# Weight splits beside the second block's tiles, the first block's units two at a time, and the state update ahead of the head norm

## The chip, the cores and the metric

The kernel runs on one core of one Trainium2 chip. A core has five engines with instruction queues of their own that meet through semaphores: TensorE (PE, matmuls into PSUM banks), VectorE (DVE), ScalarE (ACT), GpSimd (POOL) and SyncE (SP, which here only issues DMAs). The metric is the device time of one run in microseconds (us); lower is better.

## The reference

The input x is 4 x 1024 x 512 in float32. What is computed:

```python
xn = layernorm(x)
out = x + attn(xn) + ffn(xn)
# attn: an mLSTM layer and its MLP
h_in = rmsnorm(xn, norm1_w)
q, k, v = h_in @ wq, h_in @ wk, h_in @ wv        # 8 heads, 32 columns of q and k, 64 of v
i_pre, f_pre = cap(h_in @ w_ig + b_ig), cap(h_in @ w_fg + b_fg)   # cap(z) = 15 tanh(z / 15)
Fcum = cumsum(log_sigmoid(f_pre)); Dmat = causal(Fcum[t] - Fcum[s] + i_pre[s]); m = max(Dmat)
C = (q @ k.T / sqrt(32)) * exp(Dmat - m)
h = (C / max(|sum(C)|, exp(-m))) @ v
x1 = xn + (sigmoid(h_in @ w_og) * headnorm(h) * mh_w) @ w_out
h2 = rmsnorm(x1, norm2_w)
attn = x1 + (silu(h2 @ w_gate) * (h2 @ w_up)) @ w_down            # 512 -> 2048 -> 512
# ffn: weights looked up from 16 values by index, 512 -> 1376 -> 512
ffn = (silu(xn @ lut[gate_idx].T) * (xn @ lut[up_idx].T)) @ lut[down_idx].T
```

## The kernel before

**Tiling.** The 4096 tokens are 8 blocks of 512 (four batches, two halves each). Every float32 product is made as three matmuls of parts: `hi` and `lo` (the rest that `hi` leaves) of both sides, hi x hi, hi x lo, lo x hi (`split`). ScalarE makes a `hi` by a copy to fp32r, and GpSimd or VectorE the `lo` by a subtraction.

**Stages.** A block has a *front* (gate logits, projections q/k, v and output gate into banks A and B, transposes, and the rows of the gates with two scans on VectorE), and then 16 MLP *tiles*. A tile t has on TensorE a gate pass, an up pass and the down pass of tile t-1, 12 matmuls of 512 columns each; ScalarE does tanh and `hidden_hi`, VectorE the product (`th`, `hm`), GpSimd `hidden_lo`. The tiles that run behind a block's front are those of the block before it, and between their passes stand, in tiles 0 to 7, the block's own eight recurrence *units* (128 tokens and four heads each), then the head transposes (`ho_T`), in tiles 8 and 9 the output projection, in tile 10 the transposes of h2, and at tile 15 those of the next block's input (`x_T`). The order is written out by hand in each engine's program; each step waits on counting semaphores.

**A unit.** TensorE: exponents (L723, bank A), scores (L729, bank B), values (L737 from the state `kv`, L740 from `ct`), state (L747). VectorE: mask (`ar`, L1536), weights (`ct`, L1543), `tt` and `hr` (L1551, L1554: the heads), update and state (L1562, L1567), and after every second unit the head norm (`norm_1`, L1573 to L1590), whose inverse root (`rh`) GpSimd makes before `norm_2` scales and gates `hn`. ScalarE: `qbd` (L1184) and the exponential (L1192).

**The first block** (`FIRST`) has no tiles beside its units, so they stand alone: unit after unit, and then its output projection, x1 and the second block's input transposes. Meanwhile the MLP weights are split: for each of 16 tiles a load of 768 KB (gate, up and down in one), `mlp_hi_` on ScalarE, `mlp_lo_` on GpSimd, and a store of 1.5 MB to `mlp_parts`; four of them in the first front, eight beside the units, the last four in the second block's front (`split(0)` to `split(3)`), these through the buffer `raw_gu`. The second block's tiles (`SECOND`) then reload the weights from `mlp_parts` (`load_gu`, `load_dn`, two slots of `gud`), as all later blocks do. The weights of v and the output gate (`vo_w`) share memory with the look-up's tiles (`look_w`) and are reloaded at the end of each looping block.

**The loop and the tail.** Six blocks run in a loop of three passes with two halves; beside their tiles ScalarE and VectorE look up the ghost weights (`look_up`). The tail has the last block's tiles alone and then the ghost FFN of all 8 blocks, which is matmul after matmul.

## Time and profile before

| | |
|---|---|
| Runs, median (lowest to highest) | 2609.22 us (2608.56 to 2611.22), 3 runs |
| Profiled execution: time, span | 2609.44 us, 2607.3 us |
| TensorE busy | 2458.7 us (94%) |
| VectorE, ScalarE, GpSimd busy | 1270.9 (49%), 914.5 (35%), 605.7 (23%) |
| Granted clock of TensorE, mean | 0.973 of full |
| First block's front, units, rest | 22.6 to 67.7, 68.5 to 155.8, 162.3 to 184.3 us |
| Second block's front, its tiles | 184.3 to 253.3, 262.3 to 437 us |

A granted clock of 1.0 is 2.4 GHz, and 0.5 is 1.2 GHz. Busy time of TensorE is counted in time, so the same matmuls look busier at the lower clock. A wait is told by the instruction that waited, its idle time before, and what released it.

### The profile page before, as it was taken

The page shows a single profiled execution, that of the slowest core. Times are in us where ns is not written, and L with a number is a line of the kernel's source. Part 1 is how long each engine was busy: PE and PEld are TensorE (multiplying, and loading weights), DVE is VectorE, ACT ScalarE, POOL GpSimd, SP SyncE. Part 2 cuts the span into 40 slices and gives each one's busy share as a digit, 9 for nine tenths or more (in the row PEclk, how much of TensorE's full clock was granted, in tenths as well). Part 3 has the DMA queues.
Part 4 walks back from the last instruction along what each step waited for, and adds up shares of the span by engine and source line. Part 5 has one row for each costly group of instructions (what it writes and reads, how often), then busy time and mean ns, then how long its engine had stood idle before and what let it go on. Part 6 is the DMA issues. An engine that isn't in the chain of part 4 may idle for free. (4 is left out here: it accounts for less than half of the span.)

```text
span 2607.3 us, 32285 instructions
## 1 busy us (share of the span) xinstructions
PE 2458.7 (94%) x11024; PEld 1986.6 (76%) x11024; DVE 1270.9 (49%) x2185; ACT 914.5 (35%) x1667; POOL 605.7 (23%) x498
## 2 busy tenths in 40 slices
PE   6565999999999999999999999989999999999998
PEld 5344787877777777787777777768888888888887
DVE  5552563577477467557746746754322222222222
ACT  5313212444445353544444535346211111111111
POOL 4532221222122122222213212222111111111111
PEclk9568999999999999999999999999999999999999
DMA  5534645246445544724644554476687678767865
GB/s 219 205 142 148 243 154 198 98 157 234 158 148 190 205 144 161 290 96 159 230 161 143 198 202 145 160 285 224 220 288 272 242 261 290 256 239 278 284 213 199
DMA packets 117333, 530.32 MB, mean 203 GB/s; under 512 B 11280, under 2 KB 11280, under 8 KB 80304
## 3 DMA queue, kind: packets, MB, share of 16 engines
q1 hardware_dynamic: 110544, 515.86, 55.9%
q10 hardware_dynamic: 6624, 12.32, 1.6%
q8 instruction: 96, 1.57, 0.2%
q14 instruction: 69, 0.57, 0.1%
HBM read 440.46 MB, written 87.69 MB: 203 GB/s over the span
## 5 line engine op out<-in xcount | busy, mean ns | idle before, releaser
L1814 POOL TENSOR_TENSOR hidden_lo<-hm,hidden_hi 128x512 fp32r<-128x512 f32 x216 | 287.4, 1331 | 1360.7 <-ACT hidden_hi L972 1360.7
L664 PE MATMUL gate_bank<-act_hi,gud 128*128 128x512 f32 x1728 | 580.2, 397 | 17.1 <-DMA gud<-mlp_parts 9.0
L664 PE MATMUL up_bank<-act_hi,gud 128*128 128x512 f32 x1728 | 591.9, 404 | 0.0
L664 PE MATMUL acc<-gud,hidden_hi 128*128 128x512 f32 x1728 | 541.2, 395 | 16.8 <-POOL hidden_lo L1814 16.8
L1384 DVE SCALAR_TENSOR_TENSOR th<-th,gate_bank 128x512 f32<-128x512 f32 x216 | 147.9, 685 | 516.2 <-ACT th L967 516.2
L664 PEld LDWEIGHTS gate_bank<-act_hi,gud 128*128 128x128 f32 x1728 | 326.5, 189 | 85.4 <-issue 17.9
L664 PEld LDWEIGHTS up_bank<-act_hi,gud 128*128 128x128 f32 x1728 | 324.9, 188 | 79.2 <-issue 13.5
L664 PEld LDWEIGHTS acc<-gud,hidden_hi 128*128 128x128 f32 x1728 | 318.6, 188 | 83.4 <-issue 12.2
L972 ACT ACTIVATE hidden_hi<-hm 128x512 fp32r<-128x512 f32 x216 | 135.9, 629 | 697.9 <-PE acc L664 694.8
L664 PE MATMUL gate_bank<-act_lo,gud 128*128 128x512 f32 x864 | 338.2, 391 | 0.0
L664 PE MATMUL acc<-gud,hidden_lo 128*128 128x512 f32 x864 | 337.6, 391 | 0.0
L664 PE MATMUL up_bank<-act_lo,gud 128*128 128x512 f32 x864 | 337.5, 391 | 0.0
L967 ACT ACTIVATE th<-gate_bank 128x512 f32<-128x512 f32 x216 | 128.7, 596 | 438.4 <-PE gate_bank L664 438.4
L1390 DVE SCALAR_TENSOR_TENSOR hm<-th,up_bank 128x512 f32<-128x512 f32 x216 | 148.6, 688 | 246.8 <-PE up_bank L664 243.2
L1044 ACT ACTIVATE look_w<-look_w,lt,ld 128x512 f32<-128x512 int32 x280 | 216.1, 804 | 0.0
L664 PEld LDWEIGHTS up_bank<-act_lo,gud 128*128 128x128 f32 x864 | 162.5, 188 | 45.5 <-issue 13.4
L664 PEld LDWEIGHTS gate_bank<-act_lo,gud 128*128 128x128 f32 x864 | 163.4, 189 | 33.3
L664 PEld LDWEIGHTS acc<-gud,hidden_lo 128*128 128x128 f32 x864 | 162.4, 188 | 34.3
L1379 DVE COPY_PREDICATED look_w<-look_w 128x512 f32<-128x512 int32 x228 | 182.2, 842 | 10.1 <-ACT look_w L1044 3.9
L1830 POOL TENSOR_TENSOR MX<-mhl,hm 40x1024 fp32r<-40x1024 f32 x32 | 63.6, 1986 | 164.7 <-DVE mhl L1493 156.1
L729 PE MATMUL bank_b<-qbd,qkT 128*128 128x512 f32 x128 | 73.7, 660 | 21.0 <-DVE tt L1562 18.4
L1184 ACT ACTIVATE qbd<-qkT,bdm 128x128 f32<-128x128 f32 x256 | 81.2, 390 | 3.4 <-PE bank_b L729 3.3
...
## 6 DMA issues: line engine op xcount, KB each, us to landing
gud<-mlp_parts SPq DMA_DIRECT2D x128, 1024.0 KB, 5.1
gud<-ghost_parts SPq DMA_DIRECT2D x88, 1024.0 KB, 5.7
gud<-mlp_parts SPq DMA_DIRECT2D x128, 512.0 KB, 3.8
...
mlp_parts<-gud SPq DMA_DIRECT2D x16, 1536.0 KB, 6.0
...
vo_w_hi<-vo_parts SPq DMA_DIRECT2D x12, 1024.0 KB, 5.9
vo_w_lo<-vo_parts SPq DMA_DIRECT2D x12, 1024.0 KB, 9.8
```

What stands on the lines that cost most here:

```text
L664: mm = pe.matmul(dst, l[a], r[c], start=first and k == 0 and n == 0, stop=last and k == len(lhs) - 1 and n == 2)
L729: pe.matmul(B[:], qkT[:, 1, g, toks(j)], qbd[:, :, :], start=True, stop=True)\
L967: act.activation(th[:], GB[:], ACT.Tanh, scale=0.5).then_inc(of.tanh.sem, 1)
L972: act.activation(HH[0][:], hm[:], ACT.Copy).then_inc(of.hid.sem, 1)
L1044: ins = act.activation(level_of(n, what), bit0(), ACT.Identity, bias=lt[:, 2 * what:2 * what + 1], scale=ld[:, what:what + 1])
L1184: act.activation(qbd[:, h, :], qkT[:, 0, g, j * P:(j + 1) * P], ACT.Copy, scale=bdm[:, h:h + 1]).then_inc(act_qbd.sem, 1)
L1379: dve.copy_predicated(level_of(n, lower), mask_of(n, k).bitcast(i32), level_of(n, upper)).then_inc(look_vec, 1)
L1384: dve.scalar_tensor_tensor(th[:], th[:], 1.0, GB[:], ALU.add, ALU.mult).then_inc(of.gated.sem, 1)
L1390: dve.scalar_tensor_tensor(hm[:], th[:], 0.5, UB[:], ALU.mult, ALU.mult).then_inc(of.hm.sem, 1)
L1814: pool.tensor_tensor(HH[1][:], hm[:], HH[0][:].bitcast(f32), ALU.subtract).then_inc(of.low.sem, 1)
L1830: pool.tensor_tensor(MX[0:n, :, :], mhl[0:n, j * P:(j + 1) * P].unsqueeze(1).to_broadcast([n, H, P]), hm32[0:n, 0:H].unsqueeze(2).to_broad ...
```

## The change

In the order of the program:

- **First block.** Its units run two at a time: odd units have their own banks (`ACC[0]`, `ACC[1]`) and tiles (`qbd2`, `ar2`, `ex2`, `ct2` in `first_rows`, which shares memory with `gud`). TensorE and VectorE do unit u+1's exponents and mask ahead of unit u's weights and values. The second block's LayerNorm and input transposes stand among the units. No MLP weight is split here.
- **Second block's front.** Last head transposes, output projection, x1, h2 and its transposes of the first block stand in it. Two MLP tiles are split (`split(0)`, `split(1)`).
- **Second block's tiles.** The other 14 are split in tiles 1 to 15, gate and up apart from down (`part` 0 and 1), through four raw buffers that share memory with `vo_w`; TensorE takes the split weights straight from `gud`, and the stores to `mlp_parts` follow. `vo_w` is stored early and reloaded after the tiles.
- **All blocks.** The state update stands ahead of the head norm. The inverse root of the norm stands ahead of `hidden_lo` on GpSimd. The four `x_T` stand together in tile 15 in banks B, A, gate and up. The down pass of tile 15 follows the next front's logits. In tile 10 the product stands ahead of the third and fourth h2 scaling. The wait for the stored MLP rows moves from VectorE's first step in the front to ScalarE's row copy.
- **Tail.** The first index load is issued ahead of the tail's tiles, and VectorE's wait for the last `vo_w` reload comes after the first product.

VectorE in the first block, second and third unit, before (`bank_a` and `bank_b` are A and B):

```order
L1551 TENSOR_TENSOR tt<-bank_b,rn 128x260
L1554 TENSOR_TENSOR hr<-bank_a,tt 128x260
L1573 SCALAR_TENSOR_TENSOR nm<-hr 128x8
L1576 TENSOR_TENSOR nm<-nm,rn 128x8
L1578 RECIPROCAL sm<-nm 128x8
L1582 TENSOR_TENSOR hn<-hr,sm 128x512
L1586 TENSOR_TENSOR ar<-hn 128x512
L1588 TENSOR_REDUCE nm<-ar 128x8
L1590 TENSOR_SCALAR sm<-nm 128x8
L1562 TENSOR_TENSOR tt<-bank_b,bdm 128x260
L1567 SCALAR_TENSOR_TENSOR kv<-kv,rn,tt 128x260
L1536 TENSOR_TENSOR ar<-bank_a,maskd 128x512
```

And after (`acc` is `ACC[0]` or `ACC[1]`; `first_rows` as output is `ar2` or `ct2`), third and fourth unit:

```order
L1629 TENSOR_TENSOR first_rows<-acc,maskd 128x512
L1637 TENSOR_TENSOR ct<-bank_b,ex 128x512
L1669 SCALAR_TENSOR_TENSOR nm<-hr 128x8
L1672 TENSOR_TENSOR nm<-nm,rn 128x8
L1674 RECIPROCAL sm<-nm 128x8
L1678 TENSOR_TENSOR hn<-hr,sm 128x512
L1682 TENSOR_TENSOR ar<-hn 128x512
L1684 TENSOR_REDUCE nm<-ar 128x8
L1686 TENSOR_SCALAR sm<-nm 128x8
L1646 TENSOR_TENSOR tt<-bank_b,rn 128x260
L1649 TENSOR_TENSOR hr<-bank_a,tt 128x260
L1657 TENSOR_TENSOR tt<-bank_b,bdm 128x260
```

The mask of the next unit has come ahead of this unit's weights; the head norm of the pair before now stands between weights and heads, where before it stood between heads and update.

TensorE from a block's last up pass on (the second block), before:

```order
L664 MATMUL up_bank<-act_hi,gud 128x512
L699 MATMUL bank_b<-ident,xn 128x128 x4
L699 MATMUL bank_a<-ident,xn 128x128 x4
L664 MATMUL acc<-gud,hidden_hi 128x512 x2
L664 MATMUL acc<-gud,hidden_lo 128x512
...
L664 MATMUL acc<-gud,hidden_lo 128x512
L699 MATMUL bank_b<-ident,xn 128x128 x4
L699 MATMUL bank_a<-ident,xn 128x128 x4
L664 MATMUL acc<-gud,hidden_hi 128x512 x2
L664 MATMUL acc<-gud,hidden_lo 128x512
```

And after (`gates_w` are the weights of the next block's logits):

```order
L717 MATMUL up_bank<-act_hi,gud 128x512
L752 MATMUL bank_b<-ident,xn 128x128 x4
L752 MATMUL bank_a<-ident,xn 128x128 x4
L752 MATMUL gate_bank<-ident,xn 128x128 x4
L752 MATMUL up_bank<-ident,xn 128x128 x4
L717 MATMUL acc<-gud,hidden_hi 128x512 x2
...
L717 MATMUL acc<-gud,hidden_lo 128x512
L1010 ISA
L717 MATMUL up_bank<-act_hi,gates_w_hi 16x512
L717 MATMUL up_bank<-act_lo,gates_w_hi 16x512
L717 MATMUL up_bank<-act_hi,gates_w_lo 16x512
```

The four transposes stand together, and the second row of down passes (tile 15's) has left this place for the one behind the logits.

GpSimd in the second block's tiles 8 to 10, before (`rh` is the norm's inverse root, `rs` with one column that of an x1 row):

```order
L1814 TENSOR_TENSOR hidden_lo<-hm,hidden_hi 128x512
L1766 TENSOR_TENSOR rh<-sm,half_pow 128x8
L1814 TENSOR_TENSOR hidden_lo<-hm,hidden_hi 128x512
L1766 TENSOR_TENSOR rs<-ve,half_pow 128x1 x3
L1814 TENSOR_TENSOR hidden_lo<-hm,hidden_hi 128x512
L1766 TENSOR_TENSOR rs<-ve,half_pow 128x1
```

And after (`gud` rows are splits):

```order
L1920 TENSOR_TENSOR gud<-raw_mlp,gud 128x512 x3
L1935 TENSOR_TENSOR hidden_lo<-hm,hidden_hi 128x512
L1920 TENSOR_TENSOR gud<-raw_mlp,gud 128x512 x3
L1887 TENSOR_TENSOR rs<-ve,half_pow 128x1 x3
L1935 TENSOR_TENSOR hidden_lo<-hm,hidden_hi 128x512
L1920 TENSOR_TENSOR gud<-raw_mlp,gud 128x512 x3
L1887 TENSOR_TENSOR rs<-ve,half_pow 128x1
L1935 TENSOR_TENSOR hidden_lo<-hm,hidden_hi 128x512
```

Three splits have come between every `hidden_lo` and what follows it.

The diff, cut to its core:

```diff
         def raw_slot(m):
-            return m % 2 if m < NM - 4 else 2
+            return m % 4 if m >= 2 else 4

         def raw_part(m):
-            return raw_mlp[:, m % 2, :] if m < NM - 4 else raw_gu[:, :, :].rearrange("p a n -> p (a n)")[:, 0:3 * D]
+            raw = raw_mlp[:, m % 4, :] if m >= 2 else raw_gu[:, :, :].rearrange("p a n -> p (a n)")[:, 0:3 * D]
+            return raw.rearrange("p (g n) -> p g n", g=3)
+
+        def raw_loads(m):
+            return 16 * (m + 1 if m < 2 else (m - 2) // 4 + 1)
+
+        def pick(at, u, even, odd):
+
+            return odd if here(at, FIRST) and u % 2 else even
...
+        def xt_bank(at, i):
+            return AB[i % 2] if here(at, PRE) else ACC[2 + i % 2] if here(at, FIRST) else (B, A, GB, UB)[i]
+
...
-                store_mlp(m)
-            for z in range(2):
-                sp.wait_ge(st_parts[z], 16 * (NM // 2))
-            load_gu(MLP, FIRST, 0)
+            store_vo(2)
+            wait(sp, vec_ln, FIRST, 0, f"xn{NB - 1}")
+            load_mlp(0)
+            wait(sp, vec_xT, FIRST, NB - 1, "lo")
+            store_xt(1, XH[1])
+            wait(sp, vec_x1, FIRST, NB - 1, "x1")
+            sp.dma_start(rows_of(x1_rows, 0), XN[0][:]).then_inc(st_x1, 16)
+            sp.wait_ge(mlp_lo[1], 1)
+            load_mlp(1)
+            sp.wait_ge(st_vo, 64)
+            wait(sp, pe_o, SECOND, NB - 1)
+            for m in (2, 3, 4):
+                load_mlp(m)

             def tiles(at):
                 b, half = at
                 mb = previous(at)
...
+                    if here(at, SECOND):
+                        store_gu(t)
+                        if t:
+                            store_dn(t - 1)
+                        if 2 <= t and t + 3 < NM:
+                            load_mlp(t + 3)
+                    elif t + 1 < NM:
                         load_gu(MLP, mb, t + 1)
                     elif here(at, TAIL):
...
+                if here(at, SECOND):
+                    store_dn(NM - 1)
+                    reload_vo(1)
+                    reload_vo(2)
+                    for z in range(2):
+                        sp.wait_ge(st_gu[z], 16 * NM // 2)
+                        sp.wait_ge(st_dn[z], 16 * NM // 2)
+                    load_gu(MLP, at, 0)
...
                     wait(pe, vec_hoT, at, u // 2 - 1, "lo")
                 else:
                     wait(pe, vec_unit, at, u - 1, "heads")
-                pe.matmul(A[:], AL[:, toks(j)], MX[:, g * HG:(g + 1) * HG, :], start=True, stop=True)\
+                pe.matmul(pick(at, u, A, ACC[0])[:], AL[:, toks(j)], MX[:, g * HG:(g + 1) * HG, :], start=True, stop=True)\
                     .then_inc(pe_unit.sem, 1)
                 wait(pe, act_qbd, at, u, "h3")
                 wait(pe, act_qkT, at, NB - 1, "k")
-                if u:
+                if here(at, FIRST):
+                    if u >= 2:
+                        wait(pe, vec_unit, at, u - 2, "update")
+                elif u:
...
+                if not isinstance(at[0], int):
+                    down(MLP, previous(previous(at)), NM - 1, NM - 1)
...
+                if here(at, SECOND):
+                    ho_T(FIRST, NB - 1)
                 q_k_T(at, 0)
+                proj(at, 2)
                 if here(at, SECOND):
                     for i in range(NB):
-                        h2_T(FIRST, i)
-                proj(at, 2)
+                        out_proj(FIRST, i)
                 q_k_T(at, 1)
                 proj(at, 3)

...
                     if stage and t == NM - 1:
-                        x_T(at, 0, XN[1 - at[1]])
-                        x_T(at, 1, XN[1 - at[1]])
+                        for i in range(NB):
+                            x_T(at, i, XN[1 - at[1]])
                     if t:
                         down(MLP, mb, t - 1, NM - 1)
                     for f, a in fill.get((t, 2), []):
                         f(at, a)
-                if stage:
-                    x_T(at, 2, XN[1 - at[1]])
-                    x_T(at, 3, XN[1 - at[1]])
-                    down(MLP, mb, NM - 1, NM - 1)

             pe.wait_ge(pool_const, IDENT_DONE)
             for i in range(NB):
                 x_T(PRE, i, XN[0])
             front(FIRST)
+            unit_1(FIRST, 0)
             for u in range(UNITS):
-                unit_1(FIRST, u)
+                if u + 1 < UNITS:
+                    unit_1(FIRST, u + 1)
                 unit_2(FIRST, u)
                 unit_3(FIRST, u)
-                if u in (2, 4, 6):
+                if u in (3, 5, 7):
                     ho_T(FIRST, u // 2 - 1)
-            ho_T(FIRST, NB - 1)
-            pe.wait_ge(pool_w, 2)
-            for i in range(NB):
-                out_proj(FIRST, i)
-            for i in range(NB):
-                x_T(FIRST, i, XN[1])
+                if u in (4, 5):
+                    for i in (0, 1):
+                        x_T(FIRST, 2 * (u - 4) + i, xn_first)

...
+            def mlp_hi_(m, part):
                 z = m % 2
-                act.wait_ge(ld_mlp[raw_slot(m)], 16 * (m // 2 + 1 if m < NM - 4 else m - (NM - 5)))
+                act.wait_ge(ld_mlp[raw_slot(m)], raw_loads(m))
                 if m >= 2:
-                    act.wait_ge(st_parts[z], 16 * (m // 2))
-                act.activation(W3[:, z, :, 0, :], raw_part(m).rearrange("p (g n) -> p g n", g=3), ACT.Copy).then_inc(mlp_hi, 1)
+                    act.wait_ge((st_gu, st_dn)[part][z], 16 * (m // 2))
+                    wait(act, (MLP.up, MLP.down)[part], FIRST, m - 2)
+                kinds = slice(2, 3) if part else slice(0, 2)
...
+                elif here(at, SECOND):
+                    act.wait_ge(st_x1, 16)
+                    wait(act, vec_h2, FIRST, NB - 1)
+                else:
+                    act.wait_ge(st_mlp[1 - half], b * 16)
...
+                    if t:
+                        hid(MLP, mb, t - 1)
+                        if here(at, SECOND) and t >= 2:
+                            mlp_hi_(t, 1)
+                    tanh(MLP, mb, t, stage)
                     if stage and t < UNITS:
-                        unit(t)
+                        unit(at, t)
+                    if here(at, SECOND) and 1 <= t < NM - 1:
+                        mlp_hi_(t + 1, 0)
                     if stage and t == 10:
...
+                    ho_T(FIRST, NB - 1)
+                    for i in range(NB):
+                        x1_(FIRST, i)
+                    for i in range(NB):
+                        h2_(FIRST, i)
+                    dve.wait_ge(st_x1, 16)
...
+            def units_first():
+
+                at = FIRST
+                clear_state(at)
+                unit_1(at, 0)
+                for u in range(UNITS):
+                    if u + 1 < UNITS:
+                        unit_1(at, u + 1)
+                    weights(at, u)
+                    if u in (2, 4, 6):
+                        norm_1(at, u // 2 - 1)
+                    if u in (3, 5, 7):
+                        norm_2(at, u // 2 - 1)
+                    unit_2(at, u)
+                    unit_3(at, u)
+                    if u == 1:
+                        ln_stats(at, x_raw, 1, 16)
+                    if u == 2:
+                        ln_square(at)
+                    if u == 3:
+                        ln_apply(at, xn_first, 1, x_raw)
+                    if u in (4, 6):
+                        ho_T(at, u // 2 - 2)
+                    if u in (5, 6):
+                        for i in (0, 1):
+                            x_T(at, 2 * (u - 5) + i)
+                norm_1(at, NB - 1)
+                ho_T(at, NB - 2)
+                norm_2(at, NB - 1)
+                wait(dve, vec_norm, at, NB - 1, "gated")
+                for i in range(NB):
...
                             h2_scale(at, 1)
                             h2_lo(at, 0)
-                            h2_scale(at, 2)
                             h2_lo(at, 1)
-                            h2_scale(at, 3)
-                            h2_lo(at, 2)
-                            h2_lo(at, 3)
-                    if not first:
-                        product(MLP, mb, t)
+                    product(MLP, mb, t)
+                    if not stage and t == 0:
+                        for z in range(2):
+                            dve.wait_ge(ld_vo[z], 32 + 32 * HALVES * (BATCH - 1))
+                        bit_0(at, 0)
+                    if stage and t == 10:
+                        h2_scale(at, 2)
+                        h2_scale(at, 3)
+                        h2_lo(at, 2)
+                        h2_lo(at, 3)
                     if stage and t < UNITS:
                         if t in (2, 4, 6):
-                            norm_2(t // 2 - 1)
-                        unit_2(t)
+                            norm_2(at, t // 2 - 1)
+                        unit_2(at, t)
                         if looks(at):
                             look_up(at, steps_taken(half, t))
+                        unit_3(at, t)
                         if t % 2:
-                            norm_1(t // 2)
-                        unit_3(t)
+                            norm_1(at, t // 2)
                         if t in (2, 4, 6):
...
+                for u in range(UNITS):
+                    vw_(at, u)
+                    if u in (1, 3, 5):
+                        mx_(at, u // 2 + 1)
+                    if u in (2, 4, 6):
+                        norm_root(at, u // 2 - 1)
...
+                    if stage and t in (2, 4, 6, 8):
+                        norm_root(at, t // 2 - 1)
+                    if t:
                         hid(MLP, mb, t - 1)
...
+                        if here(at, SECOND) and 1 <= t < NM - 1:
+                            mlp_lo_(t + 1, 0)
                         if t in (1, 3, 5):
-                            mx_(t // 2 + 1)
-                        if first and t < UNITS:
-                            mlp_lo_(4 + t)
-                        if first and t == 5:
-                            ln_root(at)
-                        if first and t == 7:
```

## Rows read from the trace of the kernel before

**Rows 1.** Windows: stretch, us; busy us of PE, PEld, DVE, ACT, POOL; PEclk, DMA share, GB/s.

```profile
68.00:156.00 88.00, 53.32 (x132) 31.50 (x132) 50.50 (x92) 30.17 (x56) 50.11 (x41) 0.54 0.56 209
156.00:184.00 28.00, 17.05 (x68) 13.37 (x68) 17.70 (x41) 2.88 (x5) 5.20 (x7) 0.74 0.34 129
184.00:262.00 78.00, 48.51 (x204) 36.36 (x204) 21.73 (x33) 27.04 (x48) 18.76 (x14) 0.81 0.37 130
262.00:437.00 175.00, 172.86 (x793) 141.37 (x794) 92.13 (x174) 39.57 (x80) 41.19 (x36) 0.99 0.54 192
2000.00:2200.00 200.00, 200.00 (x885) 165.77 (x884) 47.62 (x72) 30.41 (x50) 32.28 (x25) 1.00 0.77 271
```

**Rows 2.** TensorE's waits, 68 to 184: total us, times, longest.

```profile
PE bank_b L729 <- DVE tt L1562: 13.9, 4, 5.2
```

**Rows 3.** TensorE's waits, 184 to 263.

```profile
PE gate_bank L699 <- ACT qkT L1104: 11.4, 2, 9.3
PE gate_bank L664 <- DMA gud<-mlp_parts: 9.0, 1, 9.0
PE bank_b L664 <- ACT th L1121: 6.3, 1, 6.3
```

**Rows 4.** Timeline, first units: start, us, engine, line, form, [idle <- releaser].

```profile
74.62 1.23 PE L737 MATMUL bank_b<-kv,qkT 128*128 128x260 f32 x2 [0.85 <-DVE ct L1543]
77.49 0.43 DVE L1551 TENSOR_TENSOR tt<-bank_b,rn 128x260 f32<-128x260 f32 x1 [2.92 <-PE bank_a L740]
77.98 1.23 PE L747 MATMUL bank_b<-vw,kn 128*128 128x260 f32 x2 [0.52 <-DVE tt L1551]
79.25 0.43 DVE L1562 TENSOR_TENSOR tt<-bank_b,bdm 128x260 f32<-128x260 f32 x1 [0.86 <-PE bank_b L747]
79.82 1.19 PE L729 MATMUL bank_b<-qbd,qkT 128*128 128x512 f32 x1 [0.19 <-DVE tt L1562]
82.72 0.71 PE L737 MATMUL bank_b<-kv,qkT 128*128 128x260 f32 x2 [0.85 <-DVE ct L1543]
84.31 0.43 DVE L1551 TENSOR_TENSOR tt<-bank_b,rn 128x260 f32<-128x260 f32 x1 [1.64 <-PE bank_a L740]
```

**Rows 5.** Timeline, VectorE, later units of the first block.

```profile
113.81 0.43 DVE L1562 TENSOR_TENSOR tt<-bank_b,bdm 128x260 f32<-128x260 f32 x1
114.68 0.68 DVE L1536 TENSOR_TENSOR ar<-bank_a,maskd 128x512 f32<-128x512 f32 x1
...
124.00 2.46 DVE L1285 BATCH_NORM_STATS2 st<-raw_gu 128x6 f32<-128x512 f32 x4
```

**Rows 6.** Timeline, VectorE, a head norm in a looping block.

```profile
735.81 0.17 DVE L1573 SCALAR_TENSOR_TENSOR nm<-hr 128x8 f32<-128x8 f32 x1
...
737.18 1.67 DVE L1586 TENSOR_TENSOR ar<-hn 128x512 f32<-128x512 f32 x1
...
739.60 0.17 DVE L1590 TENSOR_SCALAR sm<-nm 128x8 f32<-128x8 f32 x1
```

**Rows 7.** TensorE's waits, 437 to 1741, six looping blocks.

```profile
PE acc L664 <- POOL hidden_lo L1814: 13.2, 12, 1.3
PE bank_a L699 <- DVE hn L1598: 7.2, 6, 1.3
PE bank_b L729 <- DVE tt L1562: 4.4, 6, 0.7
```

**Rows 8.** The tail's start: TensorE, SyncE's issue, and landings of DMAs issued then.

```profile
1754.49 0.76 PE L664 MATMUL gate_bank<-act_hi,gud 128*128 128x512 f32 x1 [8.18 <-DVE th L1384]
1746.53 0.32 SPq L497 DMA_DIRECT2D gud<-mlp_parts  x1
gud<-mlp_parts SPq DMA_DIRECT2D x1, 1024.0 KB, 6.4
```

**Rows 9.** GpSimd's split in 68 to 156 by line; the page's stores.

```profile
L1800 POOL TENSOR_TENSOR gud<-raw_mlp,gud 128x512 fp32r<-128x512 f32 x24 | 29.7, 1266 | 29.6 <-ACT gud L1001 29.6
...
mlp_parts<-gud SPq DMA_DIRECT2D x16, 1536.0 KB, 6.0
```

612 lines of the change are left out of this document (316 added, 296 removed).

## Prediction

> **What bounds the kernel now.** I read the busy time and clock by stretch first, then TensorE's waits in the stretches where it is not full, then the instructions in order of time there. The reader is to see three regimes. From 68 to 262 us [rows 1] TensorE is busy 53.3 of 88 us, 17.1 of 28 and 48.5 of 78, at a granted clock of 0.54, 0.74 and 0.81 on average, so that part of the busy time is itself stretched. From there to 1741 us it waits some 4 to 5 us per block of the loop [rows 7]. The rest is back to back matmuls: 885 in 200 us, 0.226 us each at full clock [rows 1]. TensorE is the bound everywhere but in the first 262 us, where the engines hand one unit of the recurrence to each other in turn, and in one place at 1746 us [rows 8]. So the value of the change lies in what it does to the first 262 us; the rest is worth some us each way.
>
> **Part 1, the first block's units.** Before, unit u+1 has its scores only after the state update of unit u, and on odd units the head norm stands between them: TensorE waits 13.9 us in all at the scores of four units, 5.2 us at most [rows 2]. After, the exponents and scores of unit u+1 are made in other banks while unit u goes on. What is left in series per unit, counted from the start S of the state matmuls at half clock [rows 4]: VectorE's update starts at S+1.27 (77.98 to 79.25); the next mask is 0.87 behind it (113.81 to 114.68, [rows 5]), the weights 0.7 behind that, 0.7 long, so the values' matmuls start near S+3.6, or at S+3.8 behind the 1.9 us of the scores that start at S+1.84 (79.82). They take 2.87 (74.62 to 77.49), and 0.49 on the next state matmuls start: 7.2 us. At full clock the values take 1.59 (82.72 to 84.31) and the update comes at about S+0.7 (the 1.23 of the state matmuls halved): 5.15 us. The units 2, 4 and 6 carry a head norm: 3.96 us in a looping block with a square that took 1.67 (735.81 to 739.77), 3.0 with that square at the 0.7 of its neighbours [rows 6]. GpSimd splits nothing beside it now, so I take 3.0. It stands behind the weights and hides under the 2.87 of the slow values; at full clock it makes the unit 6.5.
> The first state matmul comes at 75 to 77.5 us against 77.98: no weight splits lie on ScalarE ahead, but a second set of scores does. Seven more units are 4 x 5.15 + 3 x 6.5 = 40.1 us at full clock, 50.1 at half. Between them now lie the second block's LayerNorm (2.5 us of statistics [rows 5], 0.7 of what follows them, and about 2.6 for the rest), one head transpose's low part (0.7 for 512 columns, as all above) and the four of the input (0.7 each, some of them waited for), together 11 to 14 us, and 1.5 us until TensorE is through. TensorE starts the second block's front at 75 + 40.1 + 11.1 + 1.5 = 127.7 us, or 77.5 + 50.1 + 14.4 + 1.5 = 143.5. [...] I take the middle, 136, against 184.3.
> [...]
>
> **Part 2, the second block's front.** Before, from 184.3 to 253.3 us, 69.0, of which 11.4 and 6.3 are waits for ScalarE [rows 3], which itself stands at weights that have not landed: four tiles share one raw buffer. That leaves 51.3, some 6 of it half clock and a smaller wait of that kind. Then 9.0 for the reload of the first tile, which goes with its store [rows 3]. Into this front move the last head transposes (0.6) and the four output projections (48 matmuls x 0.226 = 10.9), with 28 us around them removed ahead of it (156 to 184, [rows 1]). New on ScalarE: the gate row's copy waits until the first block's x1 rows are stored. They are complete about 26 us into the front, land 4.3 to 6 us later, and TensorE reaches the transposes that need ScalarE behind it at 32: about 0 to 3 us. Then ScalarE's exponentials and four copies stand ahead of the last value copy, and TensorE waits 1.4 (0 to 3). Sum 51.3 - 6 + 11.5 + 0.7 = 57.5 with part of those two, with bounds 55 and 65. The second block's first tile starts at 136 + 57.5 = 193.5 against 262.28: **68.8 us less**, and its first pass, at half clock before (4.65 us for 12 matmuls against 2.7), **1.9 less**.
>
> **Part 3, the splits beside the second block's tiles.** Per tile ScalarE gets 1.5 us and GpSimd three subtractions of 1.27 = 3.8 us [rows 9], stored as 1.5 MB with 0.75 MB loaded. TensorE's tile is 11.1 us with a unit and 8.2 without. GpSimd's sum in a tile with a unit is 1.3 + 0.6 + 3.8 + half of 3.5 = 7.5 us, and the gate half (2.5) is due only at the next tile's start: hidden, with 2.8 us to spare in the first eight and 1.2 in the others. One place is not: in tile 10 the inverse root of the last x1 row stands behind hidden_lo and all three splits, some 9 us into the tile where 2.5 was enough; TensorE's fourth h2 transpose waits and product 10 behind it. Cost **3 us** (0 to 12, four tiles of the same kind). The store of tile t-1 must land before tile t+1 is split: 6.0 us [rows 9] of a tile's 8 to 11.
> GpSimd's splits and VectorE touch in SBUF: in the trace the square under hidden_lo took 1.67 instead of 0.69 [rows 6]. I take this as hidden, since VectorE is busy 92 of 175 us in the second block [rows 1]. The Trainium skill speaks against this part: SBUF - State Buffer, section Who interferes with whom, has the two engines share a port pair as an exclusive lock for a whole instruction. By that rule up to 42 x 1.27 = 53 us of VectorE time could be blocked; the sum with all of it on TensorE's path would be 50 us worse. The 1.67 agrees with the lock, but not with its lying on the path.
>
> **Part 4, the looping blocks.** The last down projection of a block now stands behind the next front's 12 gate matmuls (2.7 us) and finds hidden_lo ready: 6 waits of 1.25 go (half of the 12 that sum to 13.2, [rows 7]), **7.6** with the second block's 1.3. Before the tail block nothing is put between: **0.9 worse**, as four transposes come ahead of its hidden copy. The state update before the head norm takes away the 6 waits at tile 4's scores, **4.4** [rows 7]. But the mean is 0.87 later at tile 7, and the head transposes in tile 8, which wait for the norm already (7.2 over 6), wait 0.75 more: **4.5 worse**. In tile 10 product 10 goes ahead of two h2 scalings; ScalarE's copies, and behind them its look-ups and the hidden copy, are 0.55 later, where TensorE waits already (the other six of [rows 7]): **3.3 worse**. In all this part is worth 3.3 us; bounds -15 and +12, since each wait may as well vanish in a neighbour's.
>
> **Part 5, the tail.** TensorE waits 8.2 us at 1746 for VectorE, which waits for an index load issued behind the last weight reload [rows 8]. That load and the wait move away. Next is the tile's own weight load, issued at 1746.53 by the queue behind the same reload, 6.4 us to land: 1753.0, so **1.5 less** (0 to 4).
>
> **Sum.** 68.8 + 1.9 - 3 + 7.6 - 0.9 + 4.4 - 4.5 - 3.3 + 1.5 = 72.5. The profiled execution took 2609.4 us (span 2607.3), the median of the runs 2609.2, so they can be used alike: **2537 us**.
>
> **Rivals.** (A) The units stay at half clock and the front goes at the slow end: 143.5 + 65 = 208.5 at the first tile, 15 us worse, 2552. For it: 0.54 over the whole unit stretch; against it: no idle of 5 us is left there. Chance 0.20. (B) The port lock bites in the second block: one VectorE instruction on the path delayed by one split per tile, 14 x 1.27 = 18 us: 2555. For it the 1.67; against it the idle VectorE. 0.08. (C) The looping reorders cost more than they give, at the bad bound of part 4: 18 us worse, 2555. 0.10. (D) **Slower than before**: the hand-over of the two weight slots runs in series with TensorE, at each of 14 tiles: store 6.0, ScalarE 1.0, GpSimd 2.5 between the end of one tile's up pass and the split's end, 9.5 x 14 = 133 us, 2670. It decides once a slot's round takes longer than two tiles (22 us, or 16 without units) by 10 us. Against it: 6.0 + 1.5 + 3.8 = 11.3. 0.02. (E) The change doesn't shorten the chain, since both units need the same VectorE: then only the removed weight waits count, 17.7 and the smaller one of 3, 9.0, 1.9 and part 4's 3.3, about 35 us, 2574. For it: VectorE is busy in most of the chain; against it: the 3.7 to 5.2 us waits were of order. 0.05. My forecast 0.55.
>
> **Numbers.** The range for 8 in 10: down to 2518 (start of the front at 127.7, front 55, no cost in part 3, half of part 4's good bound) and up to 2572 (A and B or C together, just short of E). A measurement of this kernel tells 0.2%, 5 us. All but D are far below it: faster 0.97, within 0.2% 0.01, slower 0.02.
>
> **What would show it.** Right: TensorE's first matmul of a second-block tile near 193 us; units 5 to 7 us apart; the second front without an idle over 3 us; no wait for hidden_lo at the starts of fronts; tile 8 waits near 1.9 us; a wait of 5 to 7 us on a weight load near 1675. Wrong: the second block's 16 tiles taking over 185 us (175 before, [rows 1]), waits on gud or on weight stores there, or a unit spacing of 9 us or more.

## The result and the profile after

| | Before | After |
|---|---|---|
| Median (lowest to highest) | 2610.22 us (2608.56 to 2611.59), 4 runs | 2562.76 us (2561.16 to 2565.87), 4 runs |
| Ratio, 95% interval | | 0.982 (0.9803 to 0.9837) |
| Span of the profiled execution | 2607.3 us | 2561.2 us |
| Mean granted clock | 0.973 | 0.982 |

The change gives 47.5 us; 72.5 were forecast. Of all executions reported here two were far slower than their like, one of e2 (3730 us) and one of the kernel before beside e9 to e12 (11867 us), and the medians leave them out. The two profiles are 46.1 us apart, which falls on the stretches as follows. Each row runs from one landmark on TensorE (the first matmul of a block's front, or of its tiles) to the next.

| Stretch | Before | After | Difference | Forecast |
|---|---|---|---|---|
| To the second block's front | 184.3 | 134.3 | -50.1 | -48.3 |
| That front, to the first tile | 77.9 | 55.3 | -22.7 | -20.5 |
| Second block's tiles and next front | 214.1 | 222.4 | +8.3 | about 0 |
| Three first halves of loop passes, with the front behind | 651.0 | 654.5 | +3.5 | |
| Two second halves, with the loop's jump back | 435.9 | 445.6 | +9.7 | |
| The last second half, without a front | 177.3 | 183.0 | +5.7 | |
| The six halves together | 1264.3 | 1283.1 | +18.8 | -2.0 |
| The rest | 866.6 | 866.2 | -0.4 | -1.5 |

So the large terms came out 4 us better than forecast, and 27 us were lost again in blocks that were forecast to be even or 2 us better.

Busy time by stretch of the kernel after (columns as in [rows 1]): its units, its second front, the second block's tiles, and the tail at rest.

```profile
66.00:134.00 68.00, 43.98 (x146) 28.99 (x147) 45.74 (x98) 18.26 (x47) 21.51 (x18) 0.70 0.15 57
134.00:189.50 55.50, 54.55 (x259) 43.21 (x258) 35.35 (x68) 23.65 (x45) 11.71 (x11) 0.96 0.10 36
189.50:370.00 180.50, 171.23 (x783) 138.27 (x782) 100.98 (x175) 61.32 (x112) 99.10 (x80) 0.99 0.60 222
2000.00:2200.00 200.00, 200.00 (x884) 165.66 (x883) 52.12 (x80) 30.15 (x49) 31.89 (x25) 1.00 0.74 258
```

The reader sees the clock among the units at 0.70 against 0.54 [rows 1], and the second front dense at 54.6 of 55.5 us. The second block's tiles have no such cover: 9 us of idle in 180.5. TensorE's waits there, and then from 437 us on (total us, times, longest), the latter answering to [rows 7, 8]:

```profile
PE bank_a L752 <- DVE hn L1694: 3.6, 1, 3.6
PE bank_a L752 <- DVE ct L1512: 3.1, 1, 3.1
PE bank_b L808 <- DVE tt L1646: 2.6, 4, 0.7
...
PE bank_a L752 <- DVE hn L1694: 18.2, 6, 3.2
PE acc L717 <- POOL hidden_lo L1935: 12.1, 8, 2.2
PE up_bank L717 <- issue: 5.6, 2, 2.9
PE gate_bank L717 <- DMA gud<-mlp_parts: 5.1, 1, 5.1
```

The waits for the scores of tile 4 are gone (4.4 before). Those for hidden_lo went from 15.4 to 12.1, both with one of 2.2 at the end of the program (13.2 to 9.9 without it). But the head transposes of tile 8 wait 18.2 us in six blocks, 7.2 before, and two waits at the loop's jump take 5.6 (1.9 before). A long wait can also cost more than its length. TensorE behind the wait in tile 8 of a looping block after the change (before, this wait took 1.32 us in first halves and 1.08 in second ones; now it takes 2.85 and 3.20):

```profile
509.00 0.65 PE L752 MATMUL bank_a<-ident,hn 128*128 128x128 f32 x4 [2.85 <-DVE hn L1694]
...
511.17 0.63 PE L717 MATMUL acc<-gud,hidden_lo 128*128 128x512 f32 x1
...
513.83 0.39 PE L717 MATMUL bank_b<-out_w_hi,act_hi 128*128 128x512 f32 x1
```

A record of one matmul of 512 columns takes 0.63 where the clock is 1.2 GHz and 0.39 where it is 2.4. From the head transposes to the next output projection it takes 4.83 us. In experiment e1, where the wait is 1.19, the same instructions run from 719.17 to 722.41, 3.24 us, at full clock. So 1.6 us of half clock hang on this wait. All six of these waits (2.85 to 3.21 us) have the like behind them, a granted clock of 0.76 to 0.78 over the next 7 us. It doesn't hang on every wait of this length, though: behind the one of 3.63 in the second block's tile 8 the clock is 1.00.

VectorE and GpSimd on the way to one of these waits, after (tile 7 into tile 8 of another looping block; two listings joined):

```profile
719.06 0.43 DVE L1657 TENSOR_TENSOR tt<-bank_b,bdm 128x260 f32<-128x260 f32 x1 [1.06 <-PE bank_b L808]
721.29 0.69 DVE L1682 TENSOR_TENSOR ar<-hn 128x512 f32<-128x512 f32 x1
722.99 1.64 POOL L1887 TENSOR_TENSOR rh<-sm,half_pow 128x8 f32<-128x8 f32 x1 [9.96 <-DVE sm L1686]
724.59 1.26 POOL L1935 TENSOR_TENSOR hidden_lo<-hm,hidden_hi 128x512 fp32r<-128x512 f32 x1
724.66 1.74 DVE L1690 TENSOR_TENSOR hn<-hn,rh 128x512 f32<-128x512 f32 x1 [1.75 <-POOL rh L1887]
727.25 0.65 PE L752 MATMUL bank_a<-ident,hn 128*128 128x128 f32 x4 [3.20 <-DVE hn L1694]
```

VectorE stands idle for 1.06 us in front of the update, since TensorE's state matmul comes late in the tile, and the norm queues behind both. The square, 1.67 before [rows 6], is 0.69 now. But GpSimd's root (`rh`) stands ahead of hidden_lo, so hidden_lo runs beside the scaling of hn, and that takes 1.74 (0.69 in e3).

### The profile page after: what moved, and what is told of

Its sections match the earlier page's. It is cut to its first block, busy times and chain, and to the rows that moved or that the text cites. A ratio compares the mean times of both kernels' runs of the same rounds, so it can differ in the third digit from the quotient of the medians.

```text
span 2561.2 us, 32283 instructions
## 1 busy us (share of the span) xinstructions
PE 2452.6 (96%) x11024; PEld 1986.0 (78%) x11024; DVE 1256.8 (49%) x2189; ACT 915.4 (36%) x1683; POOL 602.7 (24%) x498
## 3 DMA queue, kind: packets, MB, share of 16 engines
q1 hardware_dynamic: 109344, 495.94, 54.6%
## 4 chain that ended last, share of the span: by engine, by line
PE 60%; issue 27%; POOL 7%; DVE 3%; ACT 1%; DMA 1%; POOLq 0%; DVEq 0%; SPq 0%; ACTq 0%
PE acc L717 17%; PE up_bank L717 16%; PE gate_bank L717 15%; PE bank_b L717 4%; PE bank_a L717 4%; POOL hidden_lo L1935 2%; POOL MX L1944 1%; POOL vw L1959 1%; POOL rh L1887 1%; PE gate_bank L752 1%; DVE hn L1690 0%; ACT ex L1243 0%; POOL rs L1887 0%; PE bank_b L790 0%; POOL look_w L1926 0%
## 5 line engine op out<-in xcount | busy, mean ns | idle before, releaser
L717 PE MATMUL acc<-gud,hidden_hi 128*128 128x512 f32 x1728 | 550.4, 400 | 12.1 <-POOL hidden_lo L1935 12.1
L1935 POOL TENSOR_TENSOR hidden_lo<-hm,hidden_hi 128x512 fp32r<-128x512 f32 x216 | 282.1, 1306 | 1115.5 <-ACT hidden_hi L1047 1115.5
L717 PEld LDWEIGHTS acc<-gud,hidden_hi 128*128 128x128 f32 x1728 | 325.7, 192 | 80.9 <-issue 15.7
L1887 POOL TENSOR_TENSOR rh<-sm,half_pow 128x8 f32<-128x8 f32 x32 | 52.4, 1637 | 277.3 <-DVE sm L1686 277.3
```

The lines of the kernel that those rows point to most:

```text
L717: mm = pe.matmul(dst, l[a], r[c], start=first and k == 0 and n == 0, stop=last and k == len(lhs) - 1 and n == 2)
L1887: pool.tensor_tensor(dst, src, half_pow[:, 0:n], ALU.pow).then_inc(stage.sem, 1)
L1935: pool.tensor_tensor(HH[1][:], hm[:], HH[0][:].bitcast(f32), ALU.subtract).then_inc(of.low.sem, 1)
```

## Experiments

Each experiment was timed against the kernel before, which had medians of 2610.3, 2611.3 and 2609.9 us in the three groups (e1 to e4, e5 to e8, e9 to e12). The ratio is that to the kernel before of the same group. Where the intervals of two kernels overlap, as e1's does with those of e5, e6 and e8, their medians alone don't part them, and what is said of their difference rests on the waits and block lengths in the profiles.

| | Median, us | Ratio to before, 95% |
|---|---|---|
| after | 2562.8 | 0.982 (0.9803 to 0.9837) |
| e1 norm before update in tile 7 | 2541.8 | 0.9737 (0.9721 to 0.9753) |
| e2 units one by one | 2570.9 | 0.9858 (0.9839 to 0.9878) |
| e3 root behind hidden_lo | 2562.9 | 0.9821 (0.9804 to 0.9837) |
| e4 down pass ahead of head transposes | 2549.9 | 0.9768 (0.9752 to 0.9784) |
| e5 e1, x1 root ahead of splits | 2537.4 | 0.972 (0.9703 to 0.9736) |
| e6 e1, reload later | 2546.7 | 0.9751 (0.9735 to 0.9768) |
| e7 e1, boundary | 2553.7 | 0.9779 (0.9762 to 0.9795) |
| e8 norm also before look-up | 2535.8 | 0.9712 (0.9693 to 0.973) |
| e9 e5 and e8 | 2533.4 | 0.9705 (0.9687 to 0.9722) |
| e10 e9, MX earlier | 2533.0 | 0.97 (0.9682 to 0.9717) |
| e11 before, update first alone | 2641.7 | 1.0117 (1.0099 to 1.0135) |
| e12 e9, both reloads behind the store | 2528.7 | 0.9682 (0.9664 to 0.9699) |

**e1: the head norm of tile 7.**

```diff
                         unit_2(at, t)
                         if looks(at):
                             look_up(at, steps_taken(half, t))
+                        if t == 7:
+                            norm_1(at, t // 2)
                         unit_3(at, t)
-                        if t % 2:
+                        if t in (1, 3, 5):
                             norm_1(at, t // 2)
```

> In tile 7 of every block VectorE makes the last head norm (norm_1) ahead of the state update again; all else as in the changed kernel. Theory (the wait in tile 8 is long because the norm now stands behind the update, which itself waits 1.06 us for TensorE's state matmul, and after a wait of 2.9 to 3.6 us TensorE runs at half clock for about 4 us, which costs another 1.5 us): the norm comes 2.05 us earlier, the wait in tile 8 falls from 3.2 to about 1.1 us, no half clock behind it, 7 x 3.5 = 25 us less: about 2538 us. Rival 1 (the wait counts, the half clock doesn't): 7 x 2.05 = 14 us less, 2549. Rival 2 (GpSimd's root or hidden_lo is late next and takes the place of the wait): within 3 us of 2563.

Measured: 2541.8, 21 us less. The waits of the six looping blocks:

```profile
PE acc L717 <- POOL hidden_lo L1937: 10.0, 7, 2.2
PE up_bank L717 <- issue: 9.0, 2, 4.8
PE bank_a L752 <- DVE hn L1694: 7.8, 6, 1.4
```

The wait in tile 8 fell from 18.2 to 7.8, and the tiles of a first half went from 176.0 to 173.0 us: 1.4 by the wait (2.85 to 1.42) and 1.6 by the clock. That is the theory, half clock included, and more than rival 1 had. In the second block the wait fell from 3.63 to 0.83 and the tiles by 3.1 us; there was no half clock there to win back. The 4 us short of the theory went for the most part into the two waits at the loop's jump, 5.6 to 9.0, which nobody had expected.

**e2: units one by one.**

```diff
-            unit_1(FIRST, 0)
             for u in range(UNITS):
-                if u + 1 < UNITS:
-                    unit_1(FIRST, u + 1)
+                unit_1(FIRST, u)
                 unit_2(FIRST, u)
```

(and the same on VectorE.)

> The first block's units run one after the other again (exponents, scores and mask of unit u+1 behind the state matmul and update of unit u); the second bank and tiles for odd units, the missing weight splits and the LayerNorm among the units stay. Theory (the ahead unit is what shortens the chain: mask 0.7, exponential 0.6 and weights 0.7 us, and the scores at half clock 1.9, come back into it): 2 to 3.5 us on each of 7 units, 14 to 25 us more than the changed kernel, 2577 to 2588, and a lower granted clock among the units. Rival (both units need the same VectorE, so the gain came from the splits' absence on GpSimd and ScalarE): at most 6 us more, 2569 or less.

Measured: 2570.9, 8 us more than after; the second front starts at 141.6 instead of 134.3 us, with a clock of 0.60 among the units instead of 0.70.

```profile
66.00:141.50 75.50, 49.13 (x147) 31.94 (x148) 48.80 (x98) 18.08 (x48) 21.76 (x18) 0.60 0.15 53
```

Between the two, and nearer the rival's 6: running two at a time gives 7.3 us here and not 14 or more, and that start moves by up to 3 us between profiles of kernels that are alike so far (see e6). Of the 50 us gained to this point, some 43 are there without it. 28 of these are the stretch of output projections and transposes between idle [rows 1], which has moved to other places. No run takes the other 15 apart: the splits that left GpSimd and ScalarE, and the new order, are candidates.

**e3: GpSimd's root behind hidden_lo in tile 8.**

```diff
-                    if stage and t in (2, 4, 6, 8):
+                    if stage and t in (2, 4, 6):
                         norm_root(at, t // 2 - 1)
                     if t:
                         hid(MLP, mb, t - 1)
+                    if stage and t == 8:
+                        norm_root(at, t // 2 - 1)
```

> On GpSimd the inverse root of the last head norm stands behind hidden_lo of tile 7 again, as before the change; all else as in the changed kernel. Theory (with the root first, hidden_lo runs beside VectorE's scaling of hn and stretches it from 0.69 to 1.74 us): hidden_lo is over before the norm's sums are there, the scaling takes 0.69, the wait in tile 8 falls by 1.05 to about 2.15 us: 7 us less in 7 blocks, and up to 10 more if TensorE's clock stays full behind a wait of that length: 2546 to 2556. Rival (the root is made later behind hidden_lo, by up to 1.3 us, and nothing was stretched): up to 9 us more, 2572.

Measured: 2562.9, no change. VectorE's scaling in tile 8:

```profile
726.53 0.69 DVE L1690 TENSOR_TENSOR hn<-hn,rh 128x512 f32<-128x512 f32 x1 [1.75 <-POOL rh L1887]
```

The stretch is gone, as the theory had it, but the norm itself is 0.5 us later behind an update that now has hidden_lo beside it. The six waits sum to 16.0 instead of 18.2. In the first of the blocks the clock stayed full (174.3 us of tiles), in others it still fell (175.6 and 175.9 in the first halves). Three things took the gain back: the second block's tiles grew from 180.2 to 182.7 us, as its wait in tile 8 went from 3.63 to 4.58 with half clock behind it, the waits at the jump from 5.6 to 7.9, and the tail's wait for its weight load from 5.1 to 6.1.

**e4: the down pass ahead of the head transposes.**

```diff
-                    fill[8, 1] = [(ho_T, NB - 1)]
-                    fill[8, 2] = [(out_proj, 0)]
-                    fill[9, 0] = [(out_proj, 1)]
+                    fill[8, 2] = [(ho_T, NB - 1)]
+                    fill[9, 0] = [(out_proj, 0), (out_proj, 1)]
```

> In tile 8 TensorE makes the down pass of tile 7 (2.7 us) ahead of the last head transposes, which wait for the norm, and the first output projection goes behind the gate pass of tile 9; the other engines' programs are as in the changed kernel. Theory (the wait of 3.2 us and the half clock behind it are what the looping blocks lost): 2.7 us of the wait are filled and the 1.5 at half clock are gone, 7 x 4.2 = 29 us less, 2534. Rival (x1, h2 and the transposes in tile 10 depend on the first output projection, which is 2.7 us later): the waits in tile 10 grow by as much, the sum is 5 to 10 us less, 2553 to 2558.

Measured: 2549.9, 13 us less, between the two. The rival's mechanism isn't what held it back: tile 10 waits 1.3 us, as in after. TensorE in tile 8 of a second half (1.60 in the first halves):

```profile
721.38 0.70 PE L717 MATMUL acc<-gud,hidden_hi 128*128 128x512 f32 x2 [1.96 <-POOL hidden_lo L1934]
```

The down pass needs hidden_lo, and hidden_lo stands behind the root, which waits for the same norm. So with the change's order on GpSimd this way past the norm waits for it too.

**e5: the x1 root ahead of the splits (with e1).** On GpSimd, in the second block's tile 10 (its place behind the splits goes):

```diff
+                        if here(at, SECOND) and t == 10:
+                            x1_root(at, 3)
                         if here(at, SECOND) and 1 <= t < NM - 1:
                             mlp_lo_(t + 1, 0)
```

> Beside the edit of e1, in the second block's tile 10 GpSimd makes the last inverse root of x1 ahead of its three weight splits instead of behind them. Theory (that place is why TensorE waits 3.13 us at the h2 transposes there, with half clock behind it): the wait goes, 3.1 + 1.5 = 4.6 us less than e1's 2541.8, about 2537; in the profile the second block's tiles take 172.5 instead of 177.1 us. Rival (the wait is ScalarE's and VectorE's h2 work, which also waits for other things): the block stays at 176 to 177 us and the time at 2541.

Measured: 2537.4, and 172.5 us for the second block's tiles: as the theory said. The chain that it cuts, in after: the splits, the root behind them, and TensorE behind both (two listings joined).

```profile
316.81 3.75 POOL L1920 TENSOR_TENSOR gud<-raw_mlp,gud 128x512 fp32r<-128x512 f32 x3 [5.01 <-ACT gud L1078]
320.51 0.54 POOL L1887 TENSOR_TENSOR rs<-ve,half_pow 128x1 f32<-128x1 f32 x1
322.32 1.09 PE L752 MATMUL bank_a<-ident,ex 128*128 128x128 f32 x4 [3.13 <-DVE ct L1512]
```

With it gone the block with splits beside its tiles (172.5) is no slower than before the change (174.7, of which 1.9 were half clock in its first pass) or than a looping block (173.0). TensorE's waits in it are 3.3 us in all: 0.8 in tile 8 and four of 0.5 to 0.7 at the state matmuls, where the block had one of 0.5 before. VectorE still shows the contention, as in this row of e5 in tile 10, 0.69 elsewhere:

```profile
316.99 1.78 DVE L1518 TENSOR_TENSOR act_lo<-ct,act_hi 128x512 fp32r<-128x512 f32 x1
```

**e6: the reload behind the down pass (with e1).** On SyncE, in tile 15:

```diff
+                            if half == 1:
+                                wait(sp, MLP.down, mb, NM - 2)
+                                sp.sem_inc(sp_passed, 1)
                             reload_vo(1)
```

> Beside the edit of e1, the queue of SyncE issues the first 2 MB reload of the v and output gate weights in the second half of a loop pass only when TensorE is through with the down pass of tile 14, some 9 us later than in e1. Theory (TensorE's branch at the loop's end is reached 3.3 us before its last matmul ends, and what it then waits for, 7.1 and 7.7 us in e1 against 3.8 and 3.4 in the kernel before, stands behind the bulk loads and the store in the DMA engines): the branch takes 4 us or less, the idle of 4.1 and 4.8 us at the two back-edges shrinks to about 1 us, and the half clock behind goes: 2 x 5 = 10 us less, about 2532. Rival (the branch takes long for another reason, such as what TensorE finished just before): both idles stay over 4 us, the time is that of e1 or up to 3 us more for a later landing.

Measured: 2546.7, 5 us more than e1. At the jump the theory's direction held. TensorE's branch there, as the trace's record has it (duration in ns least, median, most; the least is the loop's last pass, which doesn't jump), first e1, then e6:

```profile
L1010 PEldq COMPARE_BRANCH  x3: 83/7120/7743, 793.5 to 1665.5; - x3
```

```profile
L1013 PEldq COMPARE_BRANCH  x3: 83/4572/4987, 796.0 to 1663.5; - x3
```

The idle behind it fell from 9.0 to 3.7 us over two jumps. But at the tail the wait for a weight load, queued behind the delayed reload, rose from 5.0:

```profile
PE gate_bank L720 <- DMA gud<-mlp_parts: 13.2, 1, 13.2
```

Another 2.0 came at the transposes of a front, and this run's first block was 3.0 us longer than e1's (the start of the second front lies between 134.1 and 137.1 us in the ten profiles of kernels that are the same up to there).

**e7: the boundary (with e1).** On TensorE, for second halves (the down pass behind the next front's logits, and the one ahead of the tail, go in return):

```diff
                     if stage and t == NM - 1:
-                        for i in range(NB):
+                        for i in range(2 if at[1] == 1 else NB):
                             x_T(at, i, XN[1 - at[1]])
...
+                if stage and at[1] == 1:
+                    x_T(at, 2, XN[1 - at[1]])
+                    x_T(at, 3, XN[1 - at[1]])
+                    down(MLP, mb, NM - 1, NM - 1)
```

> Beside the edit of e1, TensorE ends the second halves of the loop (and the second block) as in the kernel before: two input transposes, the down pass of tile 14, the other two, and the down pass of tile 15 ahead of the branch; between the two halves of a pass the order of the changed kernel stays. Theory (the deferred down pass saves a wait of 1.25 us but lets TensorE reach the branch while the bulk loads run; with the old order the branch comes 4 to 5 us later, as they land): each of two back-edges costs 1.25 + 1.2 in place of 4.1 to 4.8 + 1.5 us, the tail's boundary 1.25 in place of 2.2 + 1.5, the second block's boundary 1.25 more: 7 to 8 us less than e1, 2534. Rival (the loads keep their distance to the branch, since look-ups and stores follow the same tiles): the idle stays, and the waits for hidden_lo come on top: 2 to 4 us more, 2545.

Measured: 2553.7, 12 us more than e1, beyond the rival. The waits for hidden_lo ahead of the last down pass are 2.7 us each, and not 1.25 as before the change: ScalarE's program, which this edit leaves alone, copies all four transposes ahead of the hidden tile. So e7 is not the old boundary. It shows that with ScalarE's new order the deferred down pass is the better one. At the jump 2.7 and 3.8 us remain; the branch takes 6.6 and 6.3 us, with the DMA engines at 0.94 and 0.96.

**e8: the norm also ahead of the look-up.**

```diff
                         unit_2(at, t)
+                        if t == 7:
+                            norm_1(at, t // 2)
                         if looks(at):
                             look_up(at, steps_taken(half, t))
                         unit_3(at, t)
-                        if t % 2:
+                        if t in (1, 3, 5):
                             norm_1(at, t // 2)
```

> In tile 7 VectorE makes the last head norm right behind the heads, ahead of the look-up steps (1.9 us in the looping blocks) and of the update. Theory (the norm stands on the path to tile 8's head transposes with all its length): the wait there, 1.2 to 1.4 us in e1, is gone in the looping blocks, 6 x 1.3 = 8 us less than e1, 2534. Rival 1 (GpSimd's hidden_lo or the state update is late in its place): 2 to 4 us less, 2538 to 2540. Rival 2 (the look-ups, 2 us later, hold up ScalarE's look-up chain and with it the hidden copies): as slow as e1 or slower.

Measured: 2535.8, 6 us less than e1. The waits in tile 8 fall from 7.8 to 2.9 us, so some 0.5 us of each is left of what was to be gone.

**e9 to e12.** e9 joins e5 and e8.

> The edits of e5 and e8 together: VectorE's last head norm ahead of the look-up and the update in tile 7, and the last x1 root ahead of the splits in the second block. Theory (the two waits stand in different blocks and tiles): the gains add, 4.4 and 6.0 us below e1's 2541.8: about 2531.5. Rival (with tile 8 shorter the h2 chain of tile 10 becomes late sooner): 2533 to 2536.

Measured: 2533.4, 4.0 less than e5 and 2.4 less than e8. The intervals part it from neither. The block durations add as the theory has it (172.5 for the second block, 172.1 for a first half); the first block was 1.8 us longer in this profile than in e8's.

e10, beside e9's edits, on GpSimd among the first block's units:

```diff
-                    if u in (1, 3, 5):
+                    if u in (0, 2, 4):
                         mx_(at, u // 2 + 1)
```

> As e9, and beside it, among the first block's units, GpSimd makes the factors MX of the next two units one unit earlier, ahead of the head norm's root and the LayerNorm's root. Theory (TensorE waits 3.43 and 1.09 us for MX at the exponents there, the first with half clock behind it): 3.4 + 1.1 and up to 1.5 of clock, 4 to 6 us less than e9, 2526 to 2528; the second front starts at about 129 us. Rival (VectorE, with the LayerNorm's steps, the norm and the mask, is late next, since it stands in the same chain): at most 2 us less.

Measured: 2533.0, no gain clear of noise. The wait for MX (4.5 us in after) is gone, and the one for VectorE's weights has grown from 3.65 to 5.23 at the same unit: the rival. The second front starts at 133.7 us, and not at 129.

```profile
86.94 1.24 PE L798 MATMUL bank_b<-kv,qkT 128*128 128x260 f32 x2 [5.23 <-DVE ct L1637]
```

e11, the kernel before with one part of the change:

```diff
+                        unit_3(t)
                         if t % 2:
                             norm_1(t // 2)
-                        unit_3(t)
```

> The kernel before with one part of the change alone: VectorE makes the state update ahead of the head norm, in all blocks, and nothing else moves. Theory (in tile 7 the norm then stands behind the wait for TensorE's state matmul, as the changed kernel's trace shows): tile 8's wait grows from 1.1 to 1.3 to 2.7 us with 1.5 us of half clock behind it in most blocks, tile 4's wait of 0.74 goes: 2.2 us more in each of 6 looping blocks, 3 more in the second, some 6 less among the first block's units: about 10 us slower than before, 2620. Rival (the terms of the forecast: 0.74 gained at tile 4 and 0.75 lost at tile 8 cancel, and the first block gains 6): 2604.

Measured: 2641.7, slower by 1.2% (0.99 to 1.35). The theory had the sign and a third of the size. Waits of the six looping blocks:

```profile
PE bank_a L699 <- DVE hn L1598: 16.0, 6, 2.7
...
PE bank_b L737 <- DVE ct L1543: 10.2, 18, 0.6
```

Beside the wait in tile 8 there are 18 of 0.57 us at the values, for VectorE's weights. In the changed kernel, where the root stands earlier on GpSimd, they don't occur; that the root's place is the reason is likely, and no run tests it alone. A first half's tiles take 181.8 instead of 177.6 us, the second block's 181.7 instead of 174.7; the first block gains 2.8.

e12, beside e9's edits, on SyncE:

```diff
-                            reload_vo(1)
+                            if half == 0:
+                                reload_vo(1)
...
                             sp.sem_inc(sp_passed, 1)
+                            if half == 1:
+                                reload_vo(1)
                             reload_vo(2)
```

> As e9, and in the second half of a loop pass SyncE issues both 2 MB reloads of the v and output gate weights behind the last store of look-up rows has landed, instead of one ahead of it. Theory (TensorE's branch at the loop's end is slow while bulk loads run): the store lands in 4 us and not 7, the branch is reached with little under way: its time falls from 7.2 to 7.7 to under 5 us, the idle from 4.3 to 4.7 to under 2 at both back-edges, 5 to 8 us less there; at the tail, whose first weight load is queued behind both reloads, up to 8 us more than e9 as in e6. In sum 2529 to 2535. Rival (4 MB of loads from that moment on collide with the branch all the same): the idles stay, and the tail's cost comes on top: 2538.

Measured: 2528.7, the fastest of all, 34 us below after, though its interval overlaps e9's. The branch takes 5.2 us both times against 7.6 and 6.6 in e9, and the idle falls from 8.3 to 4.5:

```profile
L1013 PEldq COMPARE_BRANCH  x3: 83/5216/5217, 789.2 to 1652.2; - x3
...
PE up_bank L720 <- issue: 4.5, 2, 2.2
```

## Why the prediction was right in kind and 25 us off in size

**Part 2 held, and of Part 1 the sum, but not the chain.** The first second-block tile starts at 189.5 us (forecast 193.5), its front takes 55.3 (57.5) with one wait of 1.0, and the units' end gives 134.3 (136). The forecast's own sign for the chain, units 5 to 7 us apart, came out once in seven:

```profile
74.23 0.71 PE L808 MATMUL bank_b<-vw,kn 128*128 128x260 f32 x2 [0.52 <-DVE tt L1646]
79.24 0.71 PE L808 MATMUL acc<-vw,kn 128*128 128x260 f32 x2 [0.52 <-DVE tt L1646]
88.66 1.23 PE L808 MATMUL bank_b<-vw,kn 128*128 128x260 f32 x2 [0.52 <-DVE tt L1646]
98.29 0.71 PE L808 MATMUL acc<-vw,kn 128*128 128x260 f32 x2 [0.52 <-DVE tt L1646]
106.44 1.24 PE L808 MATMUL bank_b<-vw,kn 128*128 128x260 f32 x2 [0.98 <-DVE tt L1646]
115.40 0.71 PE L808 MATMUL acc<-vw,kn 128*128 128x260 f32 x2 [0.52 <-DVE tt L1646]
125.01 0.71 PE L808 MATMUL bank_b<-vw,kn 128*128 128x260 f32 x2 [1.88 <-DVE tt L1646]
132.51 1.24 PE L808 MATMUL acc<-vw,kn 128*128 128x260 f32 x2 [0.52 <-DVE tt L1646]
```

The first two are 5.0 us apart, at full clock, as worked out (5.15). The others are 7.5 to 9.6 apart, three of them beyond the 9 us that the forecast named as a sign of being wrong. The LayerNorm and transposes, which the sum carried apart from the units, stand between them, and so do two waits for MX, 4.5 us, that the forecast had not. At three units TensorE waits 9.6 us in all for VectorE's weights, in one of them behind the LayerNorm's statistics. From the first row to the last it takes 58.3 us, 8.3 per unit, where it was 10.9 before. That the end came within 2 us is luck in part: the forecast had 127.7 at full clock and 143.5 at half, and chose the middle. The sum also hid that the pairing itself is worth 7.3 us (e2). Rival E, that both units need the same VectorE, was nearer the truth in its mechanism than its 0.05. It was wrong in the price, as it forgot what the moved projections give.

**Part 3: the mechanism right, the size of one term wrong.** Tile 10's root behind the splits was named, at 3 us. It measured 3.13 of wait and 1.5 of clock (4.4 in e5). The sum had no term for the half clock that a wait drags behind it. The contention of rival B is there (1.78 for 0.69), but costs the block little (e5). The rule of the Trainium skill that was weighed, SBUF - State Buffer, section Who interferes with whom, fits these stretched rows: in tile 8 the scaling of hn, 0.69 us long by itself, begins beside hidden_lo and ends 0.55 us after it (726.40 and 725.85). It doesn't tell which of them matter.

**Part 4 failed at its third term**: "the head transposes in tile 8 ... wait 0.75 more: 4.5 worse". They wait 1.5 us more in first halves and 2.1 in second ones, 11.0 in the six looping blocks, with 1.6 of half clock behind each: 20.6 in place of 4.5, and the 3.6 of the second block on top, which had no such wait. Two causes were left out. The update waits 1.06 us for TensorE ahead of the norm. And hidden_lo, moved behind the root, falls on the scaling. e1 and e8 show the first cause: putting the norm back gives 21 and then 27 us. e11 shows it from the other side: the update ahead of the norm, for which the forecast had 4.4 gained and 4.5 lost in the looping blocks, costs 31 us alone, 10.2 of them as waits at the values. e3 shows that the second is real but doesn't pay by itself. The term of tile 10 went the other way: its waits for hidden_lo grew by 1.9 us in place of 3.3.

**Part 4's boundaries were only half right.** The wait of 1.25 us is gone at every boundary with a front behind it. But where the loop jumps back, TensorE waits 2.9 and 2.7 instead of 1.2 and 0.7, and its front is 1.55 us longer at half clock: 43.7 instead of 42.2. The forecast treated the jump as free. The rows on both sides, before and after:

```profile
872.20 0.40 PE L664 MATMUL up_bank<-act_hi,gates_w_hi 128*16 128x512 f32 x1 [1.23 <-issue]
```

```profile
809.21 0.40 PE L717 MATMUL up_bank<-act_hi,gates_w_hi 128*16 128x512 f32 x1 [2.85 <-issue]
```

The branch was reached at 868.1 and left at 871.9 before, at 803.0 and 808.9 after, 2.9 and 3.4 us ahead of the end of the last matmul. So it is reached a little earlier, but above all it takes longer. That the wait ahead of it is gone is not the reason by itself: in e7 the wait is back, and the branch takes 6.6 us. Later loads shorten it (e6, e12), and edits far from it move it too (6.7 and 7.1 us in e3, 5.9 and 5.7 in after). What it waits for is not settled: in e6 it took 4.6 us with the DMA engines busy at 0.13, in the kernel before 3.8 at 0.52.

The tail's boundary waits 2.2 us, 0.96 more than before as forecast (0.9), with half clock behind it. The terms so measured for the six halves are 20.6 (tile 8), -4.4 (tile 4), -3.8 and +4.2 (boundaries without and with a jump), 2.5 (tail's boundary) and 1.9 (tile 10), 21 in sum where the landmarks give 18.8; some 2 us stay unassigned.

**Part 5.** The tail waits 5.05 us for its weight load, as forecast (5 to 7); 3.1 less than before. But the half clock behind it lasts longer than before (0.73 against 0.84 in the 11 us from there), and the wait of 2.21 us ahead of the very last down pass, the same in both, is followed by half clock only after the change. Of the 3.1 us 0.4 are left.

```profile
1705.65 0.79 PE L717 MATMUL gate_bank<-act_hi,gud 128*128 128x512 f32 x1 [5.05 <-DMA gud<-mlp_parts]
```
